# A fused attention, expert and state-space block: batch 0's output projection moved into the last attention head

## The chip, the cores and the metric

The kernel runs on one core of one Trainium2 chip, in one launch. The metric is the device time of one execution in microseconds (us), and the figure for a kernel is the median over its runs. The profile has five compute engines: TensorE (PE, with its weight loads as PEld), VectorE (DVE), ScalarE (ACT), GpSimd (POOL) and SyncE (SP). In this kernel SyncE does nothing but wait and issue DMAs. Every engine works through its own instructions in order, and they meet at semaphores.

## The reference, cut to what matters

The whole computation is four residual steps on x of shape (2, 2048, 256): attention, a mixture of experts, a state-space scan, and the mixture of experts again. The change touches the end of the first step only.

```python
Q = (x @ WQ + bQ).reshape(b, n, 16, 16)      # K and V alike; x is layer-normed
Qr, Kr = Q @ WQr, K @ WKr                    # per head
A = softmax(Qr @ Kr.T / sqrt(16))            # per head, 2048 x 2048
out = (A @ V).reshape(b, n, 256)
x = x + out @ WO + bO
```

The kernel doesn't normalise A. It forms the value sums (numerators) and the sums of the probabilities (denominators) for each head and token, and multiplies the one by the inverse of the other before the product with WO. That product, "the output projection", is 4096 tokens by 256 by 256, half of it for each batch.

## The kernel before, in words

`phase_attention` works through 32 heads, 16 of batch 0 and then 16 of batch 1. Head n takes 64 steps in eight groups of eight. Each step has a 128x512 tile of scores twice: once with rows as queries (`row_score`, L786, for a later head), whose maximum VectorE takes (`maxima`, L746), and once with keys as rows (`col_half`, L816, two matmuls a step), which ScalarE turns into probabilities (L729). The probabilities are multiplied by the values of the head and summed in one PSUM bank (`values`, L833). PE runs the row scores 16 steps and one head ahead, so the last head, n = 31, has no row scores left to make and VectorE has no maxima left to take.

The column scores go through a ring of four PSUM banks (`RING = 4`, `free_bank`): PE can make step k only after ScalarE has read step k-4. In each group of eight steps PE makes four steps, runs half of the value sums of the group before (`last_values`), makes the other four steps and runs the other half.

At the end of a head ScalarE copies the bank (`drain`, L710), SyncE stores numerators and denominators to `num_dram` and `den_dram` (`store`, L605, L607), and the maxima of the next head are negated on GpSimd (`negate`), turned on PE and sent back by SyncE (`shift`, L597). GpSimd also fetches the values of a head (`fetch`, L666) and, in the last head, adds the bias bO to all of x in eight pieces (L692).

The inverses of batch 0's denominators are made in the last head: SyncE loads the denominators in head 30 (L627), VectorE takes the reciprocal in its idle time (L765), and SyncE stores it (L640).

`phase_attention_out` is a stage of its own after a barrier. For eight groups of 512 tokens, four of each batch, SyncE loads numerators (L929), ScalarE's queue loads inverses, each row of 512 repeated over the 16 partitions of its head (L952), VectorE multiplies the two (`normalise`, L959), PE makes two pairs of 128-token tiles with WO (eight matmul instructions a pair, L986), and VectorE adds each pair to x (L971). WO is loaded by GpSimd's queue (L940). The denominators of batch 1 are loaded, inverted (L964) and stored (L935) on the way, and the inverses of batch 1 are loaded after that store has landed (`inv_stored`). The next stage (experts, first part) begins behind another barrier.

Of the kernel before, what the change touches and what calls it, by code (L numbers as in the profile page):

```python
# [15 lines left out]
P = 128  # L16
# [466 lines left out]
INV = HEADS * SEQ // P  # L483


def by_parts(rows, b):

    return rows[b * HEADS:(b + 1) * HEADS, :].rearrange("h (q n) -> (h q) n", n=INV)


def phase_attention(nc, io, x_sb, v_sb, num_dram, den_dram, inv_dram, q_dram, k_dram, sums, table, head0, head0_in):
    SLOTS = 3
    NH = BATCH * HEADS
    STEPS = QC * KT
# [12 lines left out]
    with ExitStack() as ctx:  # L507
# [46 lines left out]
        den_in = m.sem("den_in")  # L554
        inverted = m.sem("inverted")
        inv_stored = m.sem("inv_stored")
        block = ctx.enter_context(nc.Block())

        def heads(eng, head):
# [27 lines left out]
        def _(sp):  # L587
# [22 lines left out]
            def head(n, s, turn, ahead):  # L610
                if ahead >= 2:


                    if not start(n):
                        sp.wait_ge(summed, v(GR * n - 1))
                    load(n + 2, (s + 2) % SLOTS)
                if not start(n):
                    store(n - 1)
                if ahead >= 1:
                    shift(n + 1, (s + 1) % SLOTS)  # L620
                if start(n):
                    sp.dma_start(table[SPARE:SPARE + P, :], zeros[:, :]).then_inc(cleared, 16)
                    clear(sums[0:2])
                    sp.dma_start(bo[:, :], row_bcast(io["bO"], D)).then_inc(bo_in, 16)
                if is_head(n, NH - 2):
                    sp.wait_ge(acc_stored, 16 * 2 * QC * HEADS)
                    sp.dma_start(den[:, :], by_parts(den_dram, 0)).then_inc(den_in, 16)  # L627

            def clear(some):
                for to in some:  # L630
# [5 lines left out]
            sp.wait_ge(zeroed, 1)  # L636
            shift(0, 0)
            heads(sp, head)
            sp.wait_ge(inverted, 1)
            sp.dma_start(by_parts(inv_dram, 0), inv[:, :]).then_inc(inv_stored, 16)  # L640
            clear(sums[2:4])
            store(NH - 1)
            sp.wait_ge(acc_stored, 16 * 2 * QC * NH)
            sp.wait_ge(cleared, 16 * (len(sums) + 1))
            sp.wait_ge(inv_stored, 16)

        @block.gpsimd
        def _(pool):
# [30 lines left out]
            def head(n, s, turn, ahead):  # L679
                if ahead >= 2:  # L680

                    if not start(n):
                        pool.wait_ge(summed, v(GR * n))
                    fetch(n + 2, (s + 2) % SLOTS)
                if ahead >= 1:
                    negate(n + 1)
                else:

                    pool.wait_ge(bo_in, 16)
                    for g in range(GROUPS):  # L690
# [48 lines left out]
        def _(dve):  # L739
# [16 lines left out]
            def head(n, s, turn, ahead):  # L756
# [3 lines left out]
                    largest(n + 1, s1)  # L760
                if ahead >= 2:
                    maxima(n + 2, s2, range(LEAD))
                if is_head(n, NH - 1):
                    dve.wait_ge(den_in, 16)
                    dve.reciprocal(inv[:, :], den[:, :]).then_inc(inverted, 1)  # L765

            maxima(0, 0, range(STEPS))
            largest(0, 0)
# [4 lines left out]
        def _(pe):  # L773
# [119 lines left out]

def phase_attention_out(nc, io, x_sb, num_dram, den_dram, inv_dram):
    HALF_HEADS = HEADS // DC
    with ExitStack() as ctx:
        m = Mem(nc, ctx, "wo")
        wo = m.sb("wo", [P, DC, D])  # L900

        num = m.sb("num", [P, DC, TOK])
        inv = m.sb("inv", [P, DC, TOK])
# [3 lines left out]
        w_in = m.sem("w_in")  # L907
        num_in = [m.sem(f"num_in{g}") for g in range(GROUPS)]
        inv_in = [m.sem(f"inv_in{g}") for g in range(GROUPS)]
        den_in = m.sem("den_in")  # L910
        inverted = m.sem("inverted")
        inv_stored = m.sem("inv_stored")
# [2 lines left out]
        added = m.sem("added")  # L915
        block = ctx.enter_context(nc.Block())

        def cols(g):
            return slice(g * GROUP, (g + 1) * GROUP)

        def rows_of(g):
            return g // QC, slice((g % QC) * GROUP, (g % QC + 1) * GROUP)
# [15 lines left out]
        @block.gpsimd  # L938
        def _(pool):
            pool.dma_start(wo[:, :, :], io["WO"].rearrange("(c p) n -> p c n", p=P)).then_inc(w_in, 16)  # L940
            pool.wait_ge(w_in, 16)

        @block.scalar
        def _(act):
            for g in range(GROUPS):
                b, at = rows_of(g)
                if g == QC:
                    act.wait_ge(inv_stored, 16)
                for c in range(DC):
                    first = b * HEADS + c * HALF_HEADS  # L950
                    src = inv_dram[first:first + HALF_HEADS, at].rearrange("h (a n) -> h a n", a=1)
                    act.dma_start(inv[:, c, cols(g)], src.to_broadcast([HALF_HEADS, DK, GROUP])).then_inc(inv_in[g], 16)  # L952

        @block.vector
        def _(dve):
            def normalise(g):
                dve.wait_ge(inv_in[g], 16 * DC)
                dve.wait_ge(num_in[g], 16 * DC)
                dve.tensor_tensor(num[:, :, cols(g)], num[:, :, cols(g)], inv[:, :, cols(g)], ALU.mult)\  # L959
                   .then_inc(normed, 1)  # L960

            normalise(0)
            dve.wait_ge(den_in, 16)
            dve.reciprocal(inv_last[:, :], den_last[:, :]).then_inc(inverted, 1)  # L964
            for g in range(GROUPS):
                if g + 1 < GROUPS:
                    normalise(g + 1)
                for j in range(2):
                    dve.wait_ge(made, 2 * g + j + 1)
                    pair = x_sb[:, g * GT + 2 * j:g * GT + 2 * j + 2, :]  # L970
                    dve.tensor_tensor(pair, pair, pO[:, (2 * g + j) % 4, :].rearrange("p (t d) -> p t d", t=2), ALU.add)\  # L971
                       .then_inc(added, 1)
            dve.wait_ge(added, 2 * GROUPS)

        @block.tensor
        def _(pe):
            pe.wait_ge(w_in, 16)
            for g in range(GROUPS):
                pe.wait_ge(normed, g + 1)
                for j in range(2):  # L980
                    if 2 * g + j >= 4:
                        pe.wait_ge(added, 2 * g + j - 3)
                    for t in range(2):
                        for c in range(DC):
                            at = g * GROUP + (2 * j + t) * P
                            mm = pe.matmul(pO[:, (2 * g + j) % 4, t * D:(t + 1) * D], num[:, c, at:at + P], wo[:, c, :],  # L986
                                           start=(c == 0), stop=(c == DC - 1))
                    mm.then_inc(made, 1)

# [1388 lines left out]
def build(nc, io, out):  # L2378
# [9 lines left out]
    with ExitStack() as ctx:  # L2388
        m = Mem(nc, ctx, "all")
        ident = m.sb("ident", [P, P])  # L2390
        x_sb = m.sb("x", [P, TILES, D])
        with ExitStack() as values:
# [5 lines left out]
            head0_in = early_mem.sem("in")  # L2398
            phase_qkv(nc, io, x_sb, v_sb, ident, q_dram, k_dram, head0, head0_in)
            phase_attention(nc, io, x_sb, v_sb, num_dram, den_dram, inv_dram, q_dram, k_dram, sums, table,  # L2400
                            head0, head0_in)
        phase_attention_out(nc, io, x_sb, num_dram, den_dram, inv_dram)
# [27 lines left out]
```

## Time and profile before

| | us |
|---|---|
| median of 3 runs | 2875.95 (2873.8 to 2881.38) |
| the profiled execution, its own time | 2875.3 |
| its span, first to last instruction | 2873.5 |
| attention from the first maxima (161.0) to the last (1428.1) | 1267.1 |
| the rest of the last head, to the last drain (1476.1) | 48.0 |
| last stores and barrier (to 1481.0) | 4.9 |
| output stage (to the last add, 1528.5) | 47.5 |

The times are counted from the start of the span. A row of the trace has the start, the time from the first start to the last end of a run of like instructions, the engine, the line, the operation with output and inputs, how many there are, and in square brackets how long the engine was idle before and what ended that. PEclk is the granted TensorE clock as a share of full speed, 1.00 for 2.4 GHz and 0.50 for 1.2 GHz. DMA share is the mean busy share of the core's 16 DMA engines.

### The profile page before, as it was taken

The page shows a single profiled execution, that of the slowest core. Times are in us where ns is not written, and L with a number is a line of the kernel's source. Part 1 is how long each engine was busy: PE and PEld are TensorE (multiplying, and loading weights), DVE is VectorE, ACT ScalarE, POOL GpSimd, SP SyncE. Part 2 cuts the span into 40 slices and gives each one's busy share as a digit, 9 for nine tenths or more (in the row PEclk, how much of TensorE's full clock was granted, in tenths as well). Part 3 has the DMA queues.
Part 4 walks back from the last instruction along what each step waited for, and adds up shares of the span by engine and source line. Part 5 has one row for each costly group of instructions (what it writes and reads, how often), then busy time and mean ns, then how long its engine had stood idle before and what let it go on. Part 6 is the DMA issues. An engine that isn't in the chain of part 4 may idle for free. (4 is left out here: it accounts for less than half of the span.)

```text
span 2873.5 us, 45573 instructions
## 1 busy us (share of the span) xinstructions
PE 2403.4 (84%) x14814; PEld 1057.4 (37%) x14814; DVE 2253.8 (78%) x3697; ACT 1695.9 (59%) x3470; POOL 971.8 (34%) x737
## 2 busy tenths in 40 slices
PE   8898999999999999999976899817566666589981
PEld 5322222222222222222226478702122222457871
DVE  7898999999999999999816734328799999683433
ACT  3257888888888888888844323316566566443330
POOL 4500000000000000000111367762699999126772
PEclk9879999999999999999987899957799999789996
DMA  4414111111111111111075289871344443236987
GB/s 160 132 44 153 50 39 36 49 50 44 33 47 49 49 35 41 49 50 39 14 221 163 69 199 282 182 118 20 75 110 113 103 113 106 89 110 165 270 217 201
DMA packets 255164, 293.70 MB, mean 102 GB/s; under 512 B 39120, under 2 KB 210448, under 8 KB 254928
## 3 DMA queue, kind: packets, MB, share of 16 engines
q1 hardware_dynamic: 213664, 235.09, 28.7%
q0 software_dynamic: 33104, 46.42, 9.0%
q10 hardware_dynamic: 8160, 9.32, 1.0%
q8 instruction: 115, 1.88, 0.3%
q14 instruction: 121, 0.99, 0.1%
HBM read 223.35 MB, written 66.75 MB: 101 GB/s over the span
## 5 line engine op out<-in xcount | busy, mean ns | idle before, releaser
L746 DVE TENSOR_REDUCE att_mx<-att_pR 128x1 f32<-128x512 f32 x2048 | 1266.5, 684 | 33.5 <-PE att_pR L786 33.1
L729 ACT ACTIVATE att_probs<-att_pS 128x512 f32<-128x512 f32 x2048 | 1064.0, 602 | 230.7 <-PE att_pS L816 230.4
L833 PE MATMUL att_pA<-att_probs,att_vh 128*17 128x512 f32 x4096 | 539.1, 598 | 12.6 <-ACT att_acc_sb L710 12.2
L816 PE MATMUL att_pS<-att_q,att_k 64*128 64x512 bf16 x1344 | 458.1, 379 | 0.5 <-DMA att_q<-att_nmT 0.3
L2299 PE MATMUL sc_pY<-sc_hc,all_ident 128*128 128x512 f32 x512 | 262.4, 637 | 126.4 <-DVE sc_hc L2256 101.4
L2165 POOL TENSOR_TENSOR sc_bh<-ssm_du,sc_b 128x1024 f32<-128x1024 f32 x128 | 297.7, 2359 | 9.4 <-DVE sc_hc L2256 4.7
L673 POOL TENSOR_TENSOR att_neg<-att_mx,att_minus 128x16 f32<-128x16 f32 x32 | 7.1, 221 | 842.4 <-DVE att_mx L754 842.4
L786 PE MATMUL att_pR<-head_k,head_q 64*128 64x512 bf16 x704 | 257.5, 403 | 14.5 <-PEq L72 7.6
L816 PE MATMUL att_pS<-head_q,head_k 64*128 64x512 bf16 (+1 forms) x1408 | 263.3, 381 | 0.2
L816 PE MATMUL att_pS<-att_qs,att_ks 64*128 64x512 bf16 x1344 | 261.3, 377 | 0.2
L786 PE MATMUL att_pR<-att_ks,att_qs 64*128 64x512 bf16 x672 | 259.3, 386 | 0.0
L786 PE MATMUL att_pR<-att_k,att_q 64*128 64x512 bf16 x672 | 258.9, 385 | 0.4 <-DVE att_mx L746 0.4
L2246 DVE TENSOR_TENSOR_SCAN sc_bh<-sc_pD,sc_carry,sc_bh 128x1024 f32<-128x1024 f32 x96 | 222.9, 2349 | 1.7 <-ACT sc_bh L2212 1.7
L2299 PEld LDWEIGHTS sc_pY<-sc_hc,all_ident 128*128 128x128 f32 x512 | 92.8, 197 | 276.2 <-DVE sc_hc L2256 138.1
L786 PEld LDWEIGHTS att_pR<-att_ks,att_qs 64*128 64x128 bf16 x672 | 62.3, 93 | 334.3 <-DVE att_mx L746 310.7
L816 PEld LDWEIGHTS att_pS<-att_q,att_k 64*128 64x128 bf16 x1344 | 123.8, 93 | 89.5 <-ACT att_probs L729 15.8
L666 POOL COPY att_vh<-all_v 128x256 f32<-128x256 f32 x32 | 12.6, 396 | 415.0 <-PE att_pA L833 415.0
L786 PEld LDWEIGHTS att_pR<-head_k,head_q 64*128 64x128 bf16 x704 | 66.2, 94 | 235.9 <-DVE att_mx L746 208.8
L833 PEld LDWEIGHTS att_pA<-att_probs,att_vh 128*17 128x17 f32 x4096 | 69.0, 95 | 142.0 <-issue 76.9
L1589 DVE TENSOR_TENSOR f2e_hh<-f2e_sg,f2e_pG 64x256 f32<-64x256 f32 x64 | 27.1, 423 | 120.0 <-ACT f2e_sg L1526 120.0
L1589 DVE TENSOR_TENSOR f1e_hh<-f1e_sg,f1e_pG 64x256 f32<-64x256 f32 x64 | 27.1, 423 | 118.9 <-ACT f1e_sg L1526 118.9
L1453 POOL DMA_INDIRECT expert_sum<-f2e_y,f2e_ids x64 | 101.4, 1584 | 28.6 <-issue 15.9
(320 smaller groups left out, 3741.9 us busy)
## 6 DMA issues: line engine op xcount, KB each, us to landing
sc_b<-scan_rows SPq DMA_DIRECT2D x128, 256.0 KB
f_wgu<-in_w_gate SPq DMA_DIRECT2D x128, 192.0 KB
f_wgu<-in_w_up SPq DMA_DIRECT2D x128, 192.0 KB
expert_sum<-att_zeros SPq DMA_DIRECT2D x4, 4224.0 KB, 21.2
f_wd<-in_w_down SPq DMA_DIRECT2D x128, 128.0 KB
sc_c<-scan_rows SPq DMA_DIRECT2D x40, 256.0 KB
head_q<-query_parts SPq DMA_DIRECT2D x132, 64.0 KB, 2.2
head_k<-key_parts SPq DMA_DIRECT2D x132, 64.0 KB, 2.2
```

The costliest lines, as they stand in the source:

```text
L666: pool.tensor_copy(vh[s][:, :, 0:DK], src.rearrange("p n t d -> p (n t) d")).then_inc(v_in, 1)
L673: pool.tensor_tensor(neg[:, :], mx[:, :], minus[:, :], ALU.mult).then_inc(neg_ready, 1)
L729: act.activation(probs[:, k % (2 * HALF), :], bank(place(k)), ACT.Exp, scale=float(DK) ** -0.5).then_inc(expd, 1)
L746: dve.tensor_reduce(mx4[s][:, k // QC, k % QC:k % QC + 1], pR[:, (s + k) % 3, :], AX.X, ALU.max).then_inc(maxed, 1)
L786: pe.matmul(pR[:, (s + k) % 3, :], q[rows, t * P:(t + 1) * P], kk[rows, c * GROUP:(c + 1) * GROUP], start=True, stop=True).then_inc(row_sc ...
L816: mm = pe.matmul(bank(place(k)), kk[rows, t * P:(t + 1) * P], q[rows, c * GROUP:(c + 1) * GROUP], start=not half, stop=bool(half))
L833: mm = pe.matmul(pA[32 * c:32 * c + DK + 1, :], vh[s][:, t, :], probs[:, (HALF * g + j) % (2 * HALF), :], start=(t == 0), stop=(t == KT - ...
L1453: pool.indirect_dma_start(out=sums[n % 2][:, :], out_offset=bass.IndirectOffsetOnAxis(ap=ids[:, n:n + 1], axis=0), in_=y[n % R][:, :], in_ ...
L1589: dve.tensor_tensor(hh[0:H, q, :, :].rearrange("p c n -> p (c n)"), sg[H:P, q, 0:2 * CAP], pG[H:P, q, CAP:3 * CAP], ALU.mult).then_inc(hh_ ...
L2165: pool.tensor_tensor(bh[k % H_RING][:, :, :], du[:, :, col(b, k)], b_sb[s][:, :].rearrange("p (a n) -> p a n", a=1).to_broadcast([P, DC, S ...
L2246: dve.tensor_tensor_scan(both, pD[:, k % D_RING, :, :].rearrange("p c n -> p (c n)"), both, 0.0 if k < STATES else carry[:, 0, n:n + 1], A ...
L2299: mm = pe.matmul(pY[:, c, :], ident[:, :], hc[hc_slot(k)][:, c, :], start=(n == 0), stop=(n == STATES - 1))
```

## The change

Batch 0's half of the output stage goes into attention. In head 18 SyncE loads batch 0's denominators and WO; in head 19 VectorE takes the reciprocal; in head 20 SyncE stores it; in heads 21 to 24 SyncE loads numerators and inverses, 512 tokens a head; in heads 22 to 25 GpSimd multiplies them. In head 31 PE makes one pair of tiles at the end of each of the eight groups (`project`), into the three PSUM banks that the row scores have left, and VectorE adds the pairs to x. The output stage keeps batch 1 alone: denominators first, then all numerators, then the store of the inverses, and then the inverses, two groups from SyncE's queue and two from ScalarE's.

```diff
@@ phase_attention, sync, head(n)
-                if is_head(n, NH - 2):
+                if is_head(n, DIVIDE):                      # DIVIDE = HEADS + 2
                     sp.wait_ge(acc_stored, 16 * 2 * QC * HEADS)
                     sp.dma_start(den[:, :], by_parts(den_dram, 0)).then_inc(den_in, 16)
+                    sp.dma_start(wo[:, :, :], io["WO"].rearrange("(c p) n -> p c n", p=P)).then_inc(wo_in, 16)
+                if is_head(n, DIVIDE + 2):
+                    sp.wait_ge(inverted, 1)
+                    sp.dma_start(by_parts(inv_dram, 0), inv[:, :]).then_inc(inv_stored, 16)
+                g = n - (DIVIDE + 3)
+                if 0 <= g < QC:
+                    if g == 0:
+                        sp.wait_ge(inv_stored, 16)
+                    for c in range(DC):
+                        load_values(sp, num, num_dram, 0, c, g * GROUP, GROUP).then_inc(sums_in[g], 16)
+                        load_inverses(sp, inv_rows, inv_dram, 0, c, g * GROUP, GROUP).then_inc(sums_in[g], 16)
...
             heads(sp, head)
-            sp.wait_ge(inverted, 1)
-            sp.dma_start(by_parts(inv_dram, 0), inv[:, :]).then_inc(inv_stored, 16)
             clear(sums[2:4])
             store(NH - 1)
@@ gpsimd, head(n), after negate(n + 1)
-                else:
+                g = n - (DIVIDE + 4)
+                if 0 <= g < QC:
+                    cols = slice(g * GROUP, (g + 1) * GROUP)
+                    pool.wait_ge(sums_in[g], 16 * 2 * DC)
+                    pool.tensor_tensor(num[:, :, cols], num[:, :, cols], inv_rows[:, :, cols], ALU.mult)\
+                        .then_inc(divided, 1)
+                if ahead == 0:
+                    pool.wait_ge(divided, QC)
@@ vector, head(n), after the maxima
-                if is_head(n, NH - 1):
+                if is_head(n, DIVIDE + 1):
                     dve.wait_ge(den_in, 16)
                     dve.reciprocal(inv[:, :], den[:, :]).then_inc(inverted, 1)
+                if is_head(n, NH - 1):
+                    for p in range(2 * QC):
+                        dve.wait_ge(made, p + 1)
+                        dve.wait_ge(biased, p // 2 + 1)
+                        pair = x_sb[:, 2 * p:2 * p + 2, :]
+                        dve.tensor_tensor(pair, pair, pR[:, p % 3, :].rearrange("p (t d) -> p t d", t=2), ALU.add)\
+                           .then_inc(added, 1)
@@ tensor
+            def project(p):
+                if p == 0:
+                    pe.wait_ge(wo_in, 16)
+                    pe.wait_ge(maxed, STEPS * NH)
+                pe.wait_ge(divided, p // 2 + 1)
+                if p >= 3:
+                    pe.wait_ge(added, p - 2)
+                for t in range(2):
+                    for c in range(DC):
+                        mm = pe.matmul(pR[:, p % 3, t * D:(t + 1) * D], num[:, c, (2 * p + t) * P:(2 * p + t + 1) * P],
+                                       wo[:, c, :], start=(c == 0), stop=(c == DC - 1))
+                mm.then_inc(made, 1)
...
                         if j % QC == 2:
                             last_values(n, s, g, j // QC)
+                        if is_head(n, NH - 1) and j == HALF - 2:
+                            project(g)
@@ phase_attention_out, sync
-            for g in range(GROUPS):
-                b, at = rows_of(g)
+            sp.dma_start(den_last[:, :], by_parts(den_dram, 1)).then_inc(den_in, 16)
+            for g in range(QC):
                 for c in range(DC):
-                    sp.dma_start(num[:, c, cols(g)], num_dram[b * D + c * P:b * D + (c + 1) * P, at])\
-                      .then_inc(num_in[g], 16)
-                if g == 0:
-                    sp.dma_start(den_last[:, :], by_parts(den_dram, 1)).then_inc(den_in, 16)
-                if g == 1:
-                    sp.wait_ge(inverted, 1)
-                    sp.dma_start(by_parts(inv_dram, 1), inv_last[:, :]).then_inc(inv_stored, 16)
+                    load_values(sp, num1, num_dram, 1, c, g * GROUP, GROUP).then_inc(num_in[g], 16)
+            sp.wait_ge(inverted, 1)
+            sp.dma_start(by_parts(inv_dram, 1), inv_last[:, :]).then_inc(inv_stored, 16)
             sp.wait_ge(inv_stored, 16)
+            for g in range(0, QC, 2):
+                for c in range(DC):
+                    load_inverses(sp, inv, inv_dram, 1, c, g * GROUP, GROUP).then_inc(inv_in[g], 16)
@@ phase_attention_out, scalar
+            act.wait_ge(inv_stored, 16)
+            for g in range(1, QC, 2):
                 for c in range(DC):
+                    load_inverses(act, inv, inv_dram, 1, c, g * GROUP, GROUP).then_inc(inv_in[g], 16)
```

`load_values` and `load_inverses` issue the same DMAs as L929 and L952, with the same shapes. VectorE's part of the output stage starts with the reciprocal and then has four groups in place of eight; PE's has four groups in place of eight; GpSimd has none.

## Rows read from the trace of the kernel before

**Rows 1.** Busy time by stage: attention's bulk, last head, output stage.

```profile
161.00:1428.10 1267.10, 1247.36 (x9877) 359.45 (x9879) 1232.55 (x2015) 1038.78 (x2029) 30.98 (x123) 0.99 0.18 49
1428.10:1476.10 48.00, 45.36 (x335) 9.36 (x331) 1.97 (x2) 42.04 (x83) 19.17 (x11) 1.00 0.58 190
...
1481.00:1528.50 47.50, 31.18 (x128) 25.79 (x128) 21.44 (x25) 0.00 (x0) 0.97 (x1) 0.82 0.60 188
```

The columns are the stretch and its length, then the busy time and count of PE, PEld, DVE, ACT and POOL, then PEclk, DMA share and GB/s.

**Rows 2.** Timeline of VectorE in one head of batch 1.

```profile
946.07 12.38 DVE L746 TENSOR_REDUCE att_mx<-att_pR 128x1 f32<-128x512 f32 x20 [0.34 <-PE att_pR L786]
958.89 22.28 DVE L746 TENSOR_REDUCE att_mx<-att_pR 128x1 f32<-128x512 f32 x36 [0.44 <-PE att_pR L786]
```

**Rows 3.** Timeline of GpSimd in the same head.

```profile
955.70 0.40 POOL L666 COPY att_vh<-all_v 128x256 f32<-128x256 f32 x1 [14.00 <-PE att_pA L833]
```

**Rows 4.** Timeline of ScalarE in the last head, two groups.

```profile
1451.50 4.03 ACT L729 ACTIVATE att_probs<-att_pS 128x512 f32<-128x512 f32 x8 [0.31 <-PE att_pS L816]
1455.84 4.03 ACT L729 ACTIVATE att_probs<-att_pS 128x512 f32<-128x512 f32 x8 [0.32 <-PE att_pS L816]
```

**Rows 5.** Timeline of PE in the last head.

```profile
1453.62 0.39 PE L816 MATMUL att_pS<-att_qs,att_ks 64*128 64x512 bf16 x2
...
1454.15 1.05 PE L833 MATMUL att_pA<-att_probs,att_vh 128*17 128x512 f32 x8
1455.14 0.39 PE L816 MATMUL att_pS<-att_q,att_k 64*128 64x512 bf16 x1
...
1456.12 1.05 PE L833 MATMUL att_pA<-att_probs,att_vh 128*17 128x512 f32 x8
...
1472.05 1.05 PE L833 MATMUL att_pA<-att_probs,att_vh 128*17 128x512 f32 x8
1473.47 1.91 PE L833 MATMUL att_pA<-att_probs,att_vh 128*17 128x512 f32 x16 [0.37 <-ACT att_probs L729]
```

**Rows 6.** Timeline of the output stage, all engines.

```profile
1481.05 29.88 ACTq L952 DMA_DIRECT2D wo_inv<-probability_inverses x16
...
1491.72 1.23 DVE L959 TENSOR_TENSOR wo_num<-wo_num,wo_inv 128x1024 f32<-128x1024 f32 x1 [51.95 <-DMA wo_inv<-probability_inverses]
...
1493.09 9.65 PE L986 MATMUL wo_pO<-wo_wo,wo_num 128*128 128x256 f32 x32 [17.71 <-DVE wo_num L959]
...
1495.00 5.67 SPq L929 DMA_DIRECT2D wo_num<-value_sums x12
...
1513.38 14.40 PE L986 MATMUL wo_pO<-wo_wo,wo_num 128*128 128x256 f32 x64 [1.84 <-DVE wo_num L959]
...
1527.82 0.69 DVE L971 TENSOR_TENSOR all_x<-all_x,wo_pO 128x512 f32<-128x512 f32 x1 [1.04 <-PE wo_pO L986]
```

**Rows 7.** Busy time by stretch of the output stage, columns as in the first group.

```profile
1495.00:1502.00 7.00, 7.00 (x27) 5.91 (x26) 2.18 (x3) 0.00 (x0) 0.00 (x0) 0.77 0.99 263
1502.00:1507.00 5.00, 3.37 (x16) 2.66 (x15) 3.91 (x5) 0.00 (x0) 0.00 (x0) 1.00 1.04 350
1507.00:1520.00 13.00, 11.11 (x51) 9.14 (x50) 7.33 (x10) 0.00 (x0) 0.00 (x0) 1.00 0.53 196
```

**Rows 8.** By source line: the reciprocal, as shortest, median, longest ns.

```profile
L765 DVE RECIPROCAL att_inv<-att_den x1: 1753/1753/1753, 1438.0 to 1438.0; 128x256 f32<-128x256 f32 x1
```

**Rows 9.** By source line: three of SyncE's small DMAs, to landing.

```profile
L627 SPq DMA_DIRECT2D att_den<-probability_sums x1: 579/579/579, 1435.7 to 1435.7; - x1
...
DMA to landing us min/median/max: 2.3/2.3/2.3
...
L640 SPq DMA_DIRECT2D probability_inverses<-att_inv x1: 338/338/338, 1445.9 to 1445.9; - x1
...
DMA to landing us min/median/max: 1.8/1.8/1.8
...
L935 SPq DMA_DIRECT2D probability_inverses<-wo_inv_last x1: 319/319/319, 1494.6 to 1494.6; - x1
...
DMA to landing us min/median/max: 6.8/6.8/6.8
```

More of the change, by code:

```diff
@@ L483, with load_values, load_inverses, phase_attention @@
 INV = HEADS * SEQ // P
+def load_values(eng, to, num_dram, b, c, at, n):
+    return eng.dma_start(to[:, c, at:at + n], num_dram[b * D + c * P:b * D + (c + 1) * P, at:at + n])
+def load_inverses(eng, to, inv_dram, b, c, at, n):
+    first, count = b * HEADS + c * (HEADS // DC), HEADS // DC
+    src = inv_dram[first:first + count, at:at + n].rearrange("h (a n) -> h a n", a=1)
+    return eng.dma_start(to[:, c, at:at + n], src.to_broadcast([count, DK, n]))
 def by_parts(rows, b):
     return rows[b * HEADS:(b + 1) * HEADS, :].rearrange("h (q n) -> (h q) n", n=INV)
-def phase_attention(nc, io, x_sb, v_sb, num_dram, den_dram, inv_dram, q_dram, k_dram, sums, table, head0, head0_in):
+def phase_attention(nc, io, x_sb, v_sb, num_dram, den_dram, inv_dram, q_dram, k_dram, sums, table, head0, head0_in,
+                    num, inv_rows, wo):
     SLOTS = 3
@@ L556, in phase_attention @@
         inv_stored = m.sem("inv_stored")
+        wo_in = m.sem("wo_in")
+        sums_in = [m.sem(f"sums_in{g}") for g in range(QC)]
+        divided = m.sem("divided")
+        made = m.sem("made")
+        added = m.sem("added")
+        DIVIDE = HEADS + 2
         block = ctx.enter_context(nc.Block())
@@ L644, in _ @@
             sp.wait_ge(cleared, 16 * (len(sums) + 1))
-            sp.wait_ge(inv_stored, 16)
+            sp.wait_ge(wo_in, 16)
         @block.gpsimd
@@ L762, in head @@
                     maxima(n + 2, s2, range(LEAD))
-                if is_head(n, NH - 1):
+                if is_head(n, DIVIDE + 1):
                     dve.wait_ge(den_in, 16)
                     dve.reciprocal(inv[:, :], den[:, :]).then_inc(inverted, 1)
+                if is_head(n, NH - 1):
[5 more added lines that the diff above has]
+                           .then_inc(added, 1)
+                    dve.wait_ge(added, 2 * QC)
             maxima(0, 0, range(STEPS))
@@ L890, in _, with phase_attention_out @@
                 values(NH - 1, (NH - 1) % SLOTS, GR - 1, half)
-def phase_attention_out(nc, io, x_sb, num_dram, den_dram, inv_dram):
-    HALF_HEADS = HEADS // DC
+def phase_attention_out(nc, x_sb, num_dram, den_dram, inv_dram, wo):
     with ExitStack() as ctx:
         m = Mem(nc, ctx, "wo")
-        wo = m.sb("wo", [P, DC, D])
-        num = m.sb("num", [P, DC, TOK])
-        inv = m.sb("inv", [P, DC, TOK])
+        num1 = m.sb("num1", [P, DC, SEQ])
+        inv = m.sb("inv", [P, DC, SEQ])
         den_last = m.sb("den_last", [P, INV])
@@ L906, in phase_attention_out @@
         pO = m.ps("pO", [P, 4, BANK])
-        w_in = m.sem("w_in")
-        num_in = [m.sem(f"num_in{g}") for g in range(GROUPS)]
-        inv_in = [m.sem(f"inv_in{g}") for g in range(GROUPS)]
+        num_in = [m.sem(f"num_in{g}") for g in range(QC)]
+        inv_in = [m.sem(f"inv_in{g}") for g in range(QC)]
         den_in = m.sem("den_in")
@@ L916, in phase_attention_out @@
         block = ctx.enter_context(nc.Block())
[L918 to L922, printed above, removed]
         @block.sync
         def _(sp):
-            for g in range(GROUPS):
-                b, at = rows_of(g)
+            sp.dma_start(den_last[:, :], by_parts(den_dram, 1)).then_inc(den_in, 16)
+            for g in range(QC):
                 for c in range(DC):
-                    sp.dma_start(num[:, c, cols(g)], num_dram[b * D + c * P:b * D + (c + 1) * P, at])\
-                      .then_inc(num_in[g], 16)
-                if g == 0:
-                    sp.dma_start(den_last[:, :], by_parts(den_dram, 1)).then_inc(den_in, 16)
-                if g == 1:
-                    sp.wait_ge(inverted, 1)
-                    sp.dma_start(by_parts(inv_dram, 1), inv_last[:, :]).then_inc(inv_stored, 16)
+                    load_values(sp, num1, num_dram, 1, c, g * GROUP, GROUP).then_inc(num_in[g], 16)
@@ L936, in _ @@
+            sp.wait_ge(inverted, 1)
+            sp.dma_start(by_parts(inv_dram, 1), inv_last[:, :]).then_inc(inv_stored, 16)
             sp.wait_ge(inv_stored, 16)
[L938 to L941, printed above, removed]
+            for g in range(0, QC, 2):
+                for c in range(DC):
+                    load_inverses(sp, inv, inv_dram, 1, c, g * GROUP, GROUP).then_inc(inv_in[g], 16)
@@ L943, in _ @@
         @block.scalar
         def _(act):
[L945 to L948, printed above, removed]
+            act.wait_ge(inv_stored, 16)
+            for g in range(1, QC, 2):
                 for c in range(DC):
-                    first = b * HEADS + c * HALF_HEADS
-                    src = inv_dram[first:first + HALF_HEADS, at].rearrange("h (a n) -> h a n", a=1)
-                    act.dma_start(inv[:, c, cols(g)], src.to_broadcast([HALF_HEADS, DK, GROUP])).then_inc(inv_in[g], 16)
+                    load_inverses(act, inv, inv_dram, 1, c, g * GROUP, GROUP).then_inc(inv_in[g], 16)
@@ L954, in _, with invert @@
         @block.vector
         def _(dve):
+            def invert():
+                dve.wait_ge(den_in, 16)
+                dve.reciprocal(inv_last[:, :], den_last[:, :]).then_inc(inverted, 1)
             def normalise(g):
+                cols = slice(g * GROUP, (g + 1) * GROUP)
                 dve.wait_ge(inv_in[g], 16 * DC)
                 dve.wait_ge(num_in[g], 16 * DC)
-                dve.tensor_tensor(num[:, :, cols(g)], num[:, :, cols(g)], inv[:, :, cols(g)], ALU.mult)\
-                   .then_inc(normed, 1)
+                dve.tensor_tensor(num1[:, :, cols], num1[:, :, cols], inv[:, :, cols], ALU.mult).then_inc(normed, 1)
@@ L962, in _ @@
+            invert()
             normalise(0)
[L963 to L966, printed above, removed]
+            for g in range(QC):
+                if g + 1 < QC:
                     normalise(g + 1)
@@ L969, in _ @@
                     dve.wait_ge(made, 2 * g + j + 1)
-                    pair = x_sb[:, g * GT + 2 * j:g * GT + 2 * j + 2, :]
+                    at = (QC + g) * GT + 2 * j
+                    pair = x_sb[:, at:at + 2, :]
                     dve.tensor_tensor(pair, pair, pO[:, (2 * g + j) % 4, :].rearrange("p (t d) -> p t d", t=2), ALU.add)\
                        .then_inc(added, 1)
-            dve.wait_ge(added, 2 * GROUPS)
+            dve.wait_ge(added, 2 * QC)
         @block.tensor
         def _(pe):
-            pe.wait_ge(w_in, 16)
-            for g in range(GROUPS):
+            for g in range(QC):
                 pe.wait_ge(normed, g + 1)
@@ L985, in _ @@
                             at = g * GROUP + (2 * j + t) * P
-                            mm = pe.matmul(pO[:, (2 * g + j) % 4, t * D:(t + 1) * D], num[:, c, at:at + P], wo[:, c, :],
+                            mm = pe.matmul(pO[:, (2 * g + j) % 4, t * D:(t + 1) * D], num1[:, c, at:at + P], wo[:, c, :],
                                            start=(c == 0), stop=(c == DC - 1))
@@ L2391, in build @@
         x_sb = m.sb("x", [P, TILES, D])
+        out_ctx = ctx.enter_context(ExitStack())
+        out_mem = Mem(nc, out_ctx, "out")
+        wo = out_mem.sb("wo", [P, DC, D])
+        num0 = out_mem.sb("num0", [P, DC, SEQ])
         with ExitStack() as values:
@@ L2398, in build @@
             head0_in = early_mem.sem("in")
+            inv_rows = early_mem.sb("inv_rows", [P, DC, SEQ])
             phase_qkv(nc, io, x_sb, v_sb, ident, q_dram, k_dram, head0, head0_in)
             phase_attention(nc, io, x_sb, v_sb, num_dram, den_dram, inv_dram, q_dram, k_dram, sums, table,
-                            head0, head0_in)
-        phase_attention_out(nc, io, x_sb, num_dram, den_dram, inv_dram)
+                            head0, head0_in, num0, inv_rows, wo)
+        phase_attention_out(nc, x_sb, num_dram, den_dram, inv_dram, wo)
+        out_ctx.close()
         ffn(nc, io, "f1", x_sb, ident, table, sums[0:2], None)
```

## The prediction

> **What bounds the kernel now.** I read the busy time by stage first, then the timeline of each engine in a head and in the last head, then the output stage with its DMA.
>
> In the bulk of attention VectorE is busy 1232.6 of 1267.1 us, 97% [rows 1]. Its reductions follow one another every 0.619 us (12.38 / 20 and 22.28 / 36) and it waits for PE twice a head, 0.34 and 0.44 us [rows 2]. PE is nearly as full, but at full clock and with short waits for VectorE's banks: VectorE sets the pace, and work added to VectorE there is paid for. GpSimd is busy 31 of 1267 us.
>
> The last head is different: no maxima are left, VectorE idles. A group of eight steps takes 4.34 us, of which ScalarE works 4.03 and waits 0.31 for PE [rows 4]. The reader should see a loop between two engines there, not one full engine. ScalarE begins a group at 1451.50; after about half of its exponentials PE gets banks for the second four steps (1453.62), runs the second half of the value sums (1454.15 to 1455.14), makes the first scores of the next group, and only then can ScalarE begin again, at 1455.84 [rows 4, 5]. Without waits PE needs 1.97 us for half a group (1454.15 to 1456.12), 3.94 for a group, so 0.40 us of the 4.34 is PE waiting [rows 5].
>
> The output stage takes 47.5 us, and PE works in 31.2 of them [rows 1]. It starts late: the first division waits for inverses until 1491.72, 10.7 us after their first issue, and PE starts at 1493.09. The first two groups take 9.65 us at a low clock, the last four 14.40 us, or 1.80 us a pair, at full clock [rows 6]. The 13 us from 1507, in which ScalarE's inverse loads were what was still being issued, show a DMA share of 0.53 and 196 GB/s; while numerators and inverses mix it is 263 to 350 GB/s at a share of 1 [rows 7]. So a repeated load uses about half of the DMA engines.
>
> **The change part by part.** Call the start of the output stage S (1481.05 before).
>
> *DMAs in heads 18 to 25.* SyncE gets 19 more: two loads in head 18, a store in 20, four loads in each of 21 to 24. At 0.47 us each (5.67 / 12, [rows 6]) that is 1.9 us a head, issued behind the shift of the next head, the only transfer of a head that is due at once. Queued behind them are the loads of two heads on, and those are not used for most of a head. The DMA share in the bulk is 0.18 [rows 1]. Their waits are for things a head old (a store that lands in 1.8 us, [rows 9]; a reciprocal of the head before). I count nothing; without that cover it would be 1.9 us in each of four heads.
>
> *Reciprocal in head 19.* 1.75 us [rows 8], until now in VectorE's idle time, now in its full queue, with the maxima of the head after behind it, and PE's row scores behind those. From below, VectorE could win back its 0.78 us of waits in a head: 0.97. From above 1.75. Its waits stand elsewhere in the head and are caused by PE's order, which is delayed with it, so I take 1.7.
>
> *Divisions in heads 22 to 25.* Four on GpSimd, of the shape of the bias additions: (19.17 - 0.66) / 8 = 2.3 us each [rows 1], on an engine that is nearly idle, behind the negation. The fetch behind them waits for PE's sums, that are several us into the next head. I count nothing; if each stopped VectorE, 9.2 us (a rival, below).
>
> *Projections in head 31.* Eight pairs at 1.80 us [rows 6]. VectorE's eight adds are 0.69 each [rows 6] on an idle engine, the banks are three, so PE doesn't wait for them. But a projection stands between the second half of the value sums and the first scores of the next group, that is inside the loop between PE and ScalarE. Then it is not set against PE's 0.40 us of waiting: ScalarE has run out and starts later by the whole 1.80. From below, if PE's waits vanish, 1.40 each. From above, the pair at the low clock, 9.65 / 4 = 2.41; the clock here is 1.00 [rows 1], so that end is far. I take 1.80 for seven. The eighth falls before the last sums, where PE waits anyway: the half at 1472.05 ends at about 1473.04 and the last begin at 1473.47 [rows 5], so 0.43 is hidden and 1.37 is paid. Sum 7 x 1.80 + 1.37 = 14.0, bounds 11.2 (7 x 1.40 + 1.37) and 18.8 (7 x 2.41 + 1.98).
>
> The Trainium skill bears on this (TensorEngine Tiling (Array Packing), Key Properties): changing the tiling mode drains TensorE, and each projection uses the whole array between two kinds of packed matmul. No row here prices that alone. An estimate from the row of the value half (1.05 us from first start to last end, the next 0.99 after the first) sees under 0.1 us a change; with 0.1 for each of eight projections the sum would be 0.8 us higher.
>
> *The output stage.* It loses four of eight groups, and its chain is rearranged. Denominators are issued at S, land after 2.3 us when alone [rows 9], say 2.6 with numerators behind; the reciprocal ends at S + 4.4. SyncE has then issued eight numerator loads (0.58 + 8 x 0.47 = 4.3) and issues the store at S + 4.4. The store took 1.8 us to land in a quiet stretch and 6.8 in this stage [rows 9], so S + 6.2 to S + 11.2. It is queued behind 2.1 MB of numerators (eight of 128 x 512 x 4 bytes), 8.0 us at 263 GB/s, begun about S + 1.5 after the denominators: I take S + 10.5. Then the inverses: two groups, 1.05 MB, at 196 GB/s are 5.4 us, with 1.1 to begin and 0.5 to land: S + 17.5. From division to PE 1.37 (1491.72 to 1493.09), then 9.65 for two groups out of the cold, 7.2 for two warm ones (half of 14.40), and the last add 0.69 [rows 6]: S + 36.4. Before, the end was 1527.82 + 0.69, S + 47.5. The stage saves 11.1.
>
> Lower end of that: denominators, numerators and two groups of inverses, 3.28 MB, at 350 GB/s [rows 7] and 1.0 to begin, are there at S + 10.4, the end is S + 29.2, saved 18.3. Upper end: the store lands at S + 11.2 and the first inverses take the 10.7 us they took before, S + 21.9, the end is S + 40.8, saved 6.7.
>
> The split of the inverses over two queues I price at nothing. If each queue had its own half of the DMA engines, two groups would land in 2.7 us and the stage would save 2.7 us more. The share of 0.53 shows one queue alone and can't tell. The Trainium skill (DMA: Bandwidth & Descriptors, Rules for kernel authors) says that a DMA whose outermost dimension has c < 16 entries is confined to at most c engines, and that spreading DMAs over issuing engines brings no bandwidth; an inverse load has eight heads outermost. By that rule both queues share the same eight, as I have it in the sum.
>
> The sum: + 14.0 (last head) + 1.7 (reciprocal) - 11.1 (output stage) = + 4.6 us. On the profiled execution's own 2875.3 that is 2879.9, call it 2880. The median of the runs shown is 2875.95, 0.65 above that execution, well inside what can be told apart.
>
> **The rivals.** A difference of 0.3%, 8.6 us, is about what a measurement of this kernel can tell from no change.
>
> *Slower: the first inverses come late.* The chain denominators, reciprocal, store, inverses is serial, where before batch 0's half covered it. If the store lands last and the first inverses again take 10.7 us, the stage saves 6.7 and the sum is + 9.0: 2884. It decides from a saving of under 7.1 us. For it: the 10.7 us is what the only row of a first inverse load shows. Against: there it shared with numerators, here they are done.
>
> *Slower: the divisions stop VectorE.* Four of 2.3 us add 9.2: 2889. Against it: GpSimd's fetch at 955.70, also out of SBUF, falls in a stretch of reductions that keep 0.619 us apart exactly as in the stretch without one [rows 2, 3]. It lasts only 0.40 us, so this isn't excluded.
>
> *Faster: the stage halves.* If half the groups are half the time, 23.7 saved, 14.0 + 1.7 - 23.7 = - 8.0: 2867. It would need the first division at S + 4.9; the reciprocal alone is over at S + 4.4. With all low ends (11.2 + 0.97 - 18.3) it is - 6.1: 2869. So a faster kernel beyond 0.3% needs something that no row shows.
>
> **How the numbers follow.** The forecast of no change that can be told, 0.70, with its likeliest time of 2880 and its own range 2871 to 2884. Late inverses 0.13 and divisions that stop VectorE 0.07 make slower 0.20. The halved stage has 0.10, which is faster. The range takes in the bounds on both sides and ends between the rivals: 2869 to 2888.
>
> **What would show it.** In the profile after, a group of the last head should take 6.1 us in place of 4.34, with ScalarE idle some 2 us before each; the last head should be 14 us longer. Head 19 should be 1.7 longer than its neighbours and heads 22 to 25 not longer. The output stage should take 36 us, with the first division about 17 to 18 us after its start and PE idle until then. It would be wrong if a group of the last head grew by only 1.4, or by more than 2; if the first division came before S + 12 or after S + 21; or if the reductions in heads 22 to 25 showed gaps of 2 us.

## The result and the profile after

The changed kernel takes 2883.57 us (median of 6 runs, 2881.73 to 2888.37) against 2875.01 (6 runs, 2871.53 to 2881.38): a ratio of 1.0027, 95% interval 1.0015 to 1.004, that is 4 to 12 us slower. Forecast were + 4.6 us, 2880, and a range of 2869 to 2888. The difference of the medians, 8.6 us, lies at the edge of what was called no change. The profiled execution takes 2881.7, 6.4 above that of before, and its stages say where the time went. Busy time by stage, columns as in [rows 1]:

```profile
162.30:1430.70 1268.40, 1247.73 (x9877) 359.70 (x9879) 1233.82 (x2016) 1038.75 (x2029) 40.29 (x127) 0.99 0.20 53
1430.70:1493.70 63.00, 60.39 (x399) 20.97 (x395) 5.73 (x9) 41.95 (x83) 19.15 (x11) 1.00 0.43 141
1498.80:1536.30 37.50, 16.41 (x64) 13.75 (x64) 11.79 (x13) 0.00 (x0) 0.00 (x0) 0.67 0.35 119
```

Against [rows 1] the bulk is 1.3 us longer, the rest of the last head 15.0 longer and the output stage 10.0 shorter: + 6.3. Two differences that no edit touches cancel: the first maxima come 1.3 later, and what follows the output stage is 1.3 shorter.

VectorE around the reciprocal of head 19, and GpSimd's fetch in that head (two timelines):

```profile
989.51 3.75 DVE L781 TENSOR_REDUCE att_mx<-att_pR 128x1 f32<-128x512 f32 x6
993.18 1.75 DVE L800 RECIPROCAL att_inv<-att_den 128x256 f32<-128x256 f32 x1
994.84 7.37 DVE L781 TENSOR_REDUCE att_mx<-att_pR 128x1 f32<-128x512 f32 x12
1002.65 0.69 DVE L781 TENSOR_REDUCE att_mx<-att_pR 128x1 f32<-128x512 f32 x1 [0.44 <-PE att_pR L829]
```

```profile
999.47 0.40 POOL L694 COPY att_vh<-all_v 128x256 f32<-128x256 f32 x1 [15.52 <-PE att_pA L876]
```

The reductions go on without a gap on either side: VectorE was the pace, and the reciprocal pushes everything back. GpSimd's wait for PE's sums in that head, 14.00 us in [rows 3], is 15.52: the head is 1.52 us longer, not 1.75. The wait behind the reductions is 0.44 us as in [rows 2], so the 0.23 us were not won back there.

A division on GpSimd in head 22, and VectorE beside it (two timelines):

```profile
1107.11 2.36 POOL L719 TENSOR_TENSOR out_num<-out_num,head_inv_rows 128x1024 f32<-128x1024 f32 x1
```

```profile
1106.23 4.95 DVE L781 TENSOR_REDUCE att_mx<-att_pR 128x1 f32<-128x512 f32 x8
```

Eight reductions in 4.95 us, 0.619 apart, as in [rows 2]: the division stops nothing.

The last head, two groups of ScalarE and one of PE (timelines, compare [rows 4, 5]):

```profile
1460.05 4.03 ACT L764 ACTIVATE att_probs<-att_pS 128x512 f32<-128x512 f32 x8 [2.24 <-PE att_pS L859]
1466.32 4.03 ACT L764 ACTIVATE att_probs<-att_pS 128x512 f32<-128x512 f32 x8 [2.24 <-PE att_pS L859]
```

```profile
1462.17 0.39 PE L859 MATMUL att_pS<-att_qs,att_ks 64*128 64x512 bf16 x2
1462.40 0.38 PE L859 MATMUL att_pS<-att_q,att_k 34*128 34x512 bf16 x1
1462.71 1.05 PE L876 MATMUL att_pA<-att_probs,att_vh 128*17 128x512 f32 x8
1463.69 1.99 PE L903 MATMUL att_pR<-out_wo,out_num 128*128 128x256 f32 x8
1465.62 0.39 PE L859 MATMUL att_pS<-att_q,att_k 64*128 64x512 bf16 x1
```

A group takes 6.27 us in place of 4.34. The projection holds PE for 1.93 us (1463.69 to 1465.62), and ScalarE's idle time before a group grows from 0.31 to 2.24, by the same 1.93. PE's own work in a group is now 3.94 + 1.93 = 5.87 us, so 0.40 of the 6.27 is still PE waiting, as much as before. From the first exponential of the last head to its last drain it is 52.7 us after and 37.9 before (1437.57 to 1475.45): + 14.8.

The output stage (timeline):

```profile
1498.79 0.35 SPq L975 DMA_DIRECT2D wo_den_last<-probability_sums  x1
1499.20 3.74 SPq L488 DMA_DIRECT2D wo_num<-value_sums  x8
1500.83 1.75 DVE L997 RECIPROCAL wo_inv_last<-wo_den_last 128x256 f32<-128x256 f32 x1 [8.87 <-DMA wo_den_last<-probability_sums]
1502.98 0.43 SPq L980 DMA_DIRECT2D probability_inverses<-wo_inv_last  x1
1509.79 2.89 SPq L495 DMA_DIRECT2D wo_inv<-probability_inverses  x4
...
1517.83 1.23 DVE L1003 TENSOR_TENSOR wo_num<-wo_num,wo_inv 128x1024 f32<-128x1024 f32 x1 [15.24 <-DMA wo_inv<-probability_inverses]
```

It is one chain: denominators 2.0 us, reciprocal 1.75, the store issued 4.2 us after the start of the stage and landed 6.8 later, the first inverses another 8.0. The first division comes at 19.0 us, and PE stands idle until 20.3. Its four groups take 16.4 us. The DMA in the stage, by stretch:

```profile
1503.00:1509.10 6.10, 0.00 (x0) 0.00 (x0) 0.00 (x0) 0.00 (x0) 0.00 (x0) 0.50 0.75 254
1511.00:1517.00 6.00, 0.00 (x0) 0.00 (x0) 0.00 (x0) 0.00 (x0) 0.00 (x0) 0.50 0.46 143
1517.00:1523.00 6.00, 3.89 (x9) 3.17 (x10) 2.52 (x3) 0.00 (x0) 0.00 (x0) 0.50 0.54 206
```

With both queues issuing inverses the share stays at 0.54, as with one in [rows 7].

### The profile page after: what moved, and what is told of

The parts are those of the page before. It is cut to its first block and busy times, and to the rows that moved or that the text cites. A ratio compares the mean times of both kernels' runs of the same rounds, so it can differ in the third digit from the quotient of the medians.

```text
span 2880.0 us, 45578 instructions
## 1 busy us (share of the span) xinstructions
PE 2406.0 (84%) x14814; PEld 1058.6 (37%) x14814; DVE 2250.5 (78%) x3693; ACT 1696.1 (59%) x3470; POOL 979.2 (34%) x740
## 5 line engine op out<-in xcount | busy, mean ns | idle before, releaser
L1495 POOL DMA_INDIRECT expert_sum<-f2e_y,f2e_ids x64 | 101.4, 1584 | 29.7 <-issue 16.4
```

What stands on the lines that cost most here:

```text
L1495: pool.indirect_dma_start(out=sums[n % 2][:, :], out_offset=bass.IndirectOffsetOnAxis(ap=ids[:, n:n + 1], axis=0), in_=y[n % R][:, :], in_ ...
```

## The experiments

Theory: the projections cost their whole time because they stand in a loop between PE and ScalarE, while PE idles at the start of the output stage. Rival: PE is full, and the same matmuls cost the same anywhere. Further runs divide the output stage's chain and the reciprocal. All start from the changed kernel, the last but one from e1. Where there is one run, its time can't tell differences of a few us, and the stages in its trace are compared.

**Projections first in the output stage (e1).**

```diff
@@ attention, last head
-                        if is_head(n, NH - 1) and j == HALF - 2:
-                            project(g)
...
@@ output stage, tensor: eight pairs of batch 0, then eight of batch 1
+            for q in range(4 * QC):
+                rows, p = ((num0, q), (num1, q - 2 * QC))[q >= 2 * QC]
+                if q >= 2 * QC:
+                    pe.wait_ge(normed, p // 2 + 1)
...
@@ output stage, vector: the adds of batch 0 after the reciprocal
+            for q in range(2 * QC):
+                add(q)
```

> Batch 0's eight projections leave the last head and stand first on PE in the output stage, before batch 1's first division; the loads and divisions in heads 18 to 25 stay. Theory (the projections cost their full 1.92 us each because they stand inside the loop between PE and ScalarE, while PE idles for 20 us at the start of the output stage): the last head goes back by 14.8 us to what it was before the change, the eight projections fit into the wait for the inverses, and batch 1's four groups run warm in 14.4 in place of 16.4 us; about 17 us less than the changed kernel, 2866 to 2868, some 8 below the kernel before. Rival (the projections are PE work that costs the same wherever it stands): the stage ends about 14 later, 2881 to 2884.

Measured: 2866.55 us (8 runs) beside 2873.57 for the kernel before (11 runs), a ratio of 0.9977, interval 0.9967 to 0.9988. It is faster than both kernels: its slowest run, 2872.77, lies below the changed kernel's fastest, 2881.73. Busy time of the rest of the last head and of the output stage, and PE's timeline in that stage:

```profile
1430.60:1478.80 48.20, 45.36 (x335) 9.42 (x331) 0.23 (x2) 42.03 (x83) 19.17 (x11) 1.00 0.55 184
1483.80:1520.30 36.50, 31.66 (x128) 26.67 (x128) 17.30 (x21) 0.00 (x0) 0.00 (x0) 0.90 0.37 123
```

```profile
1483.86 15.90 PE L1007 MATMUL wo_pO<-out_wo,out_num 128*128 128x256 f32 x64 [5.75 <-PEq L72]
1503.80 15.77 PE L1007 MATMUL wo_pO<-out_wo,wo_num 128*128 128x256 f32 x64 [4.05 <-DVE wo_num L977]
```

The last head is back at 48.2 us, and the output stage with twice the projections is 1.0 us shorter than without. The rival's 14 us more don't appear: the eight projections fit into the wait for the inverses. Only the warm start didn't hold: PE waits 4.05 us between the batches, its granted clock, 0.92 from 1503 to 1505, is 0.50 from 1505 to 1508, and batch 1 takes 15.8 us, not 14.4.

**Projection in the middle of a group (e2).** One line:

```diff
-                        if is_head(n, NH - 1) and j == HALF - 2:
+                        if is_head(n, NH - 1) and j == 2:
```

> As the changed kernel, but each projection stands after the first half of the value sums of its group (before the second four score steps), where PE waits for ScalarE, not after the second half. Theory (in the changed kernel the projection is added to a loop of PE and ScalarE, and PE's 0.4 us of waiting a group remains): the wait is filled, a group takes 3.94 + 1.92 = 5.87 us in place of 6.27, the last head is about 3 us shorter. Rival (PE is simply full in the last head, the place is nothing): a group stays at 6.27, no change.

Measured: 2882.65 us in one run, 2873.57 the median of before. ScalarE in three groups:

```profile
1460.66 4.19 ACT L764 ACTIVATE att_probs<-att_pS 128x512 f32<-128x512 f32 x8 [2.12 <-PE att_pS L859]
1466.87 4.08 ACT L764 ACTIVATE att_probs<-att_pS 128x512 f32<-128x512 f32 x8 [2.02 <-PE att_pS L859]
```

6.21 us a group, not 5.87. The expectation failed: the place gives 0.06 us, and ScalarE still waits 2.0 to 2.1 us. The next run asks whether that makes the rival right.

**Projection in two halves (e5).** `project(g, t)` makes one 128-token tile:

```diff
-                        if is_head(n, NH - 1) and j == HALF - 2:
-                            project(g)
+                        if is_head(n, NH - 1) and j % QC == 2:
+                            project(g, j // QC)
```

> As the changed kernel, but each projection is cut into its two 128-token tiles, one after each half of the value sums of the group. Theory, as it stands after the projection in the middle of the group took 6.21 us a group in place of 5.87: PE's wait only moves to the other half, because the ring of four banks lets PE run four steps ahead and ScalarE starves in whichever half holds the whole projection; with equal halves no wait of PE is left, a group takes 3.94 + 1.92 plus 0.0 to 0.1 for the second change of matmul kind, 5.86 to 5.96 us, the last head 2 to 3 us shorter than in the changed kernel. Rival (place is nothing, the projection always adds its 1.92): 6.2 to 6.3 us a group.

Measured: 2882.43 us in one run. PE in one half of a group:

```profile
1455.78 0.39 PE L859 MATMUL att_pS<-att_q,att_k 64*128 64x512 bf16 x1
...
1456.75 1.05 PE L876 MATMUL att_pA<-att_probs,att_vh 128*17 128x512 f32 x8
1457.74 1.13 PE L902 MATMUL att_pR<-out_wo,out_num 128*128 128x256 f32 x4
1458.80 0.39 PE L859 MATMUL att_pS<-att_q,att_k 64*128 64x512 bf16 x1
```

3.02 us a half, 6.04 a group, and PE goes from one kind to the next without a wait (0.97 + 0.99 + 1.06). This is PE's own limit, above the 5.96 expected and below the 6.2 of the place being nothing. The last head, from its first exponential to its last drain, is 51.5 us (1440.32 to 1491.83), 1.2 shorter than in the changed kernel and not 2 to 3. A tile of 1.06 us against 0.86 for half of a warm pair (two adds in the output stage are 1.73 apart) says that each change to the whole array and back costs 0.2 us: a projection in the last head is 1.73 of matmul and 0.2 of change. With one whole projection a group PE's work is 5.87 us, so the changed kernel keeps 0.40 us of PE's waiting and the place in the middle 0.34. The halves remove that wait and pay a second change of 0.2, which leaves a gain of 0.23.

**Store ahead of the numerators (e3).**

```diff
+            sp.wait_ge(inverted, 1)
+            sp.dma_start(by_parts(inv_dram, 1), inv_last[:, :]).then_inc(inv_stored, 16)
             for g in range(QC):
                 for c in range(DC):
                     load_values(sp, num1, num_dram, 1, c, g * GROUP, GROUP).then_inc(num_in[g], 16)
-            sp.wait_ge(inverted, 1)
-            sp.dma_start(by_parts(inv_dram, 1), inv_last[:, :]).then_inc(inv_stored, 16)
```

> As the changed kernel, but in the output stage SyncE issues the store of batch 1's inverses ahead of the eight loads of numerators. Theory (the store landed 6.8 us after its issue because it was queued behind 2 MB of numerators): it lands about 2 us after its issue, ScalarE's inverse loads start at about 6.5 us after the start of the stage in place of 11, and the stage ends 2 to 4 us sooner. Rival (6.8 us is what this store takes in this stage, queue or not): landing and end as in the changed kernel, within 1 us.

Measured: 2886.49 us in one run. The stage starts at 1497.02:

```profile
1500.93 0.34 SPq L977 DMA_DIRECT2D probability_inverses<-wo_inv_last  x1
1501.33 4.92 SPq L488 DMA_DIRECT2D wo_num<-value_sums  x8
1502.68 4.45 ACTq L495 DMA_DIRECT2D wo_inv<-probability_inverses  x4
1506.30 4.70 SPq L495 DMA_DIRECT2D wo_inv<-probability_inverses  x4
...
1520.52 2.36 DVE L1003 TENSOR_TENSOR wo_num<-wo_num,wo_inv 128x1024 f32<-128x1024 f32 x2 [19.61 <-DMA wo_inv<-probability_inverses]
```

The store lands within 1.75 us of its issue, so it was the numerators ahead of it (whether by the queue or by the DMA engines that they share, the run doesn't separate). But the first division comes 23.5 us after the start, not 19.0, and the stage is 41.2 us. SyncE now waits for the reciprocal before it issues the numerators, 4.3 us after the start in place of 0.4, and group 0's inverses stand behind them in its order, at 1506.30. So numerators and inverses share the DMA engines, and the first inverses land when the DMA has little left to do: its share is 0.2 from then on. The theory was right on the landing and wrong on the gain.

**One queue for the inverses (e6).** SyncE's loop over groups 0 and 2 is dropped, ScalarE's runs over `range(QC)`.

> As the changed kernel, but all four groups of batch 1's inverses are issued by ScalarE's queue in order, none by SyncE's. Theory (loads of both queues go through the same eight DMA engines, so two queues bring the first group later and the last no sooner): the first division comes about 2.5 us sooner, at 16 to 17 us after the start of the stage in place of 19.0, the DMA ends at the same 24 us, the stage ends about 2 us sooner. Rival (each queue brings bandwidth of its own): the first division at 19 or later, the last inverses several us later, the stage no shorter.

Measured: 2878.5 us in one run, its stage starting at 1497.03 (timeline, then busy time by stretch):

```profile
1508.70 6.46 ACTq L495 DMA_DIRECT2D wo_inv<-probability_inverses  x8
1516.31 1.23 DVE L1000 TENSOR_TENSOR wo_num<-wo_num,wo_inv 128x1024 f32<-128x1024 f32 x1 [15.47 <-DMA wo_inv<-probability_inverses]
1508.70:1516.30 7.60, 0.00 (x0) 0.00 (x0) 0.00 (x0) 0.00 (x0) 0.00 (x0) 0.50 0.34 101
```

The first division comes 19.3 us after the start, 7.6 after the issue (the store took 0.7 us longer to land than in the changed kernel). The mean rate up to it is 101 GB/s, where two queues had 128 (1509.8 to 1517.8), and the stage takes 37.5 us as there. So the theory's 2.5 us sooner didn't come, and the signs are the rival's. Its reason isn't shown: from 1515.7 to 1523.7 this one queue moves 165 GB/s at a share of 0.52, while one queue in [rows 7] moved 196 at 0.53 and two move 206 at 0.54. The runs leave open why the same half of the engines moved less here.

**GpSimd's queue for groups 1 and 3 (e7).** `@block.scalar` becomes `@block.gpsimd` over the same loop.

> As the changed kernel, but groups 1 and 3 of batch 1's inverses are issued by GpSimd's queue in place of ScalarE's. Theory (half of the DMA engines limit the repeated loads): if this queue reaches other engines, the DMA share in the inverse loads goes from 0.53 to 0.7 or more, the first division comes 2 to 4 us sooner and the DMA ends by 20 us after the start of the stage. Rival (reading the same row sixteen times is the limit, whatever the engines): the share may rise, but the rate stays near 200 GB/s and the first division near 19 us.

Measured: 2881.08 us in one run, its stage starting at 1498.50 (busy time by stretch, then timeline):

```profile
1514.50:1518.50 4.00, 0.00 (x0) 0.00 (x0) 0.19 (x1) 0.00 (x0) 0.00 (x0) 0.50 1.01 244
1518.31 2.36 DVE L1003 TENSOR_TENSOR wo_num<-wo_num,wo_inv 128x1024 f32<-128x1024 f32 x2 [16.05 <-DMA wo_inv<-probability_inverses]
```

The share is 1.01 at 244 GB/s, so other engines do work; yet the first division comes 19.8 us after the start, the first two groups together, and the DMA ends 23.7 us after the start, where the changed kernel's ends at 24.4. Nearly twice the share gave a fifth more rate, and the end came 0.7 us sooner. Of the theory only the share came true; the rival is the nearer of the two.

**The first inverses alone, on top of e1 (e8).**

```diff
+                if g == 0:
+                    sp.wait_ge(inv_in[0], 16 * DC)      # sync, in its loop over groups 0 and 2
-            act.wait_ge(inv_stored, 16)
+            act.wait_ge(inv_in[0], 16 * DC)             # scalar
```

> As the version with batch 0's projections first in the output stage, but the two inverse loads of group 0 are issued alone; groups 1 to 3 are issued, by both queues, when they have landed. In the changed kernel and the versions so far the first group landed 7.6 to 8.6 us after its issue, however the four groups were spread over queues. Theory (descriptors of the later groups are served between those of the first): alone it lands 4 to 5 us after its issue, the first division comes about 3 us sooner, at 16 us after the start of the stage, and groups 1 to 3 still come in time for PE; 1 to 3 us off the time of that version, 2863 to 2866. Rival (the first repeated load is slow by itself, as the 100 to 160 GB/s of its first 4 us suggest): it still takes 7 us or more, the first division is no sooner, the later groups come 4 us later; 2867 to 2870.

Measured: 2869.22 us (10 runs) beside 2872.42 (13 runs), a ratio of 0.9986, interval 0.9976 to 0.9996. It overlaps the interval of e1, so the times don't tell the two apart; the stage does, 39.3 us for e1's 36.5. It starts at 1482.55:

```profile
1493.12 6.56 SPq L495 DMA_DIRECT2D wo_inv<-probability_inverses  x4
1498.49 3.26 ACTq L495 DMA_DIRECT2D wo_inv<-probability_inverses  x4
1498.71 1.22 DVE L979 TENSOR_TENSOR wo_num<-wo_num,wo_inv 128x1024 f32<-128x1024 f32 x1
1507.06 1.23 DVE L979 TENSOR_TENSOR wo_num<-wo_num,wo_inv 128x1024 f32<-128x1024 f32 x1 [7.12 <-DMA wo_inv<-probability_inverses]
```

The first group lands 5.3 us after its issue (1493.12 to about 1498.4), so some 2.7 us of the 8.0 are the groups issued behind it, and the first division comes 16.2 us after the start, as the theory had it. But the other groups then take 8.6 us from their own issue and don't come in time: the second division is at 1507.06, PE stands idle from 1503.7, and its granted clock falls in that gap, from 0.98 (1505 to 1506) to 0.50 (1506 to 1508.3).

**A second reciprocal (e4).** In head 20, into a spare tile:

```diff
+                if is_head(n, DIVIDE + 2):
+                    dve.reciprocal(spare[:, :], den[:, :]).then_inc(inverted, 1)
```

> As the changed kernel, with a second reciprocal of the same size in head 20, whose result nobody reads. Theory (VectorE is the pace of the heads, a reciprocal of 1.75 us costs 1.5): head 20 is 1.5 us longer than its neighbours as head 19 is, and the time 1.5 higher. Rival (part of it is won back from VectorE's waits of 0.78 us a head): 1.0 or less.

Measured, GpSimd's fetch in head 20:

```profile
1038.95 0.40 POOL L695 COPY att_vh<-all_v 128x256 f32<-128x256 f32 x1 [15.52 <-PE att_pA L879]
```

Its wait for PE's sums is 15.52 us in head 20 too, where the same head of the changed kernel has 14.00: 1.52 once more. The one run's time, 2880.4, is below the changed kernel's median and can't resolve 1.5 us; the head does.

## Why the prediction was right, point by point

- *Last head, + 14.0.* Measured + 14.8, by the mechanism named: the projection is added whole to the loop of PE and ScalarE, and PE's 0.40 us of waiting stays. The ring decides only on that part: had the wait been filled, a group would still have grown by 5.87 - 4.34 = 1.53 us, because PE had no more to give. The pair was mis-sized by 0.13 (1.93 for 1.80): back to back it takes 1.73, and the change between kinds of matmul costs 0.2 us and not under 0.1. The rule of the Trainium skill (TensorEngine Tiling (Array Packing), Key Properties), that changing the tiling mode drains TensorE, bore more weight than the row I set against it. The runs show the 0.2 us; that a drain is their cause they don't show.
- *Reciprocal, + 1.7.* Measured + 1.5 in the head, twice. Some 0.2 us was won back, though not from the wait of 0.44 us behind the reductions; the runs don't say where.
- *Divisions and DMAs in heads 18 to 25, nothing.* Confirmed: reductions 0.619 us apart beside a division, and the bulk grew by 1.3 us, less than the reciprocal alone. The rival in which GpSimd stops VectorE is out.
- *Output stage, - 11.1.* Measured - 10.0. The store landed at 11.0 us (10.5 forecast), for the reason given, the numerators ahead of it. The first inverses took 8.0 us from their issue and not 7.0 (128 GB/s up to there, for the 196 that was carried over from a stretch in full flow), so the first division came at 19.0 in place of 17.5; PE's 16.4 us for four groups were 0.4 better. That the two queues share about half of the DMA engines is shown by the share of 0.54. The rule cited from the Trainium skill (DMA: Bandwidth & Descriptors, Rules for kernel authors), that a DMA whose outermost dimension has c < 16 entries is confined to at most c engines, agrees with that share: c is eight here. Whether spreading over two queues brings bandwidth the runs don't settle: up to the first division 101 GB/s with one queue and 128 with two, one trace each, but in full flow 196 with one in [rows 7] and 206 with two.
- *The sum, + 4.6.* The terms measured give 14.8 + 1.5 - 10.0 = + 6.3, and the profiled execution shows + 6.4. The median's + 8.6 is 2 us more, inside its interval of 4 to 12; no run attributes it.

The time was within the range, and the change is slower by what lies at the edge of 0.3%. The interval of 4 to 12 us excludes a difference of nothing, and that the median fell just inside 8.6 us is luck. What stays open is why the first half megabyte of inverses takes 5.3 us even alone.

## What to carry to other kernels

Work put "into the idle time" of an engine that is one side of a two-engine ring can cost its full length: ask how much the engine waits (here 0.40 us for 1.93 of work), and whether the work stands between what the other engine gives and what it waits for. The same eight projections cost 14.8 us in the last head and nothing in a stage where the engine waits 20 us for a serial DMA chain. So look for the longest wait that ends on something else, and move independent work there.

## What the runs showed that was not expected

A projection of matmuls on the whole array, between kinds that use parts of it, costs 0.2 us beyond its own 1.73, each time. The whole projection in the other half of the group only moves PE's wait (6.21 us a group); two equal halves remove it, but pay a second change (6.04). Issuing a small store ahead of bulk loads made it land in 1.75 us in place of 6.8 and still lengthened the stage by 3.7 us, since the bulk loads then started later and ran against the loads that the store released.
